# One joined product of v and state, and the q decay split over two engines

## The reference

```
def step(S, qkv_c):                       # one chunk: T = 128 tokens, D = 64
    qi, ki, vi = qkv_c
    scores = einsum('bhtd,bhsd,hts->bhts', qi, ki, mask)   # mask: exp(-s(t-s')) for t >= s', else 0
    intra  = einsum('bhts,bhsd->bhtd', scores, vi)
    cross  = einsum('bhtd,ht,bhde->bhte', qi, lam_t, S)    # lam_t = exp(-s t)
    o = scale * (intra + cross)
    kv = einsum('bhtd,ht,bhte->bhde', ki, lam_rev, vi)
    return (lam_T * S + kv, o)
out = rmsnorm(rmsnorm(outs, norm_w), proj_norm_w) @ weight_quant(proj_w).T
x + out * silu(ffn(layernorm(x)))
```

## Time and profile before

| | |
|---|---|
| median of 3 timed runs | 1314.46 us (1314.1 to 1314.81) |
| profiled execution, span | 1314.2 us; no time of its own is recorded beside the span |
| busy | PE 1289.1, DVE 1008.4, ACT 617.4, POOL 600.4 us |
| granted TensorE clock | full (2.4 GHz) in all 40 slices |

### The profile page before, as it was taken

How to read it: one execution, slowest core, us unless ns; L and a number is a source line. 1 busy time by engine, 2 the same in 40 slices (tenths; PEclk the granted TensorE clock), 3 DMA queues, 4 the chain that set the end, 5 groups by cost and what they waited for, 6 DMA issues and landing times.

```text
span 1314.2 us, 25908 instructions
## 1 busy us (share of the span) xinstructions
PE 1289.1 (98%) x10263; PEld 824.8 (63%) x10263; DVE 1008.4 (77%) x1567; ACT 617.4 (47%) x1216; POOL 600.4 (46%) x537
## 2 busy tenths in 40 slices
PE   4999999999999999999999999999999999999998
PEld 2577767675665757566574656657566575756655
DVE  7888367687676887878788787877878788787755
ACT  5884144344434635446354544644436363544621
POOL 1442785955354435354432535435333443535352
PEclk9999999999999999999999999999999999999999
DMA  9631101203012030210303011030300304021020
GB/s 361 248 97 66 57 34 37 101 33 106 1 38 100 17 121 18 76 46 18 121 17 120 18 57 65 17 121 18 94 28 19 119 17 121 17 58 49 1 65 32
DMA packets 33433, 90.32 MB, mean 69 GB/s; under 512 B 10529, under 2 KB 10785, under 8 KB 33314
## 3 DMA queue, kind: packets, MB, share of 16 engines
q1 hardware_dynamic: 33024, 88.65, 20.0%
q10 hardware_dynamic: 290, 0.02, 0.0%
HBM read 71.85 MB, written 16.81 MB: 67 GB/s over the span
## 4 chain that ended last, share of the span: by engine, by line
PE 94%; DVE 2%; ACT 2%; DMA 1%; issue 1%; SPq 0%; POOL 0%; DVEq 0%; ACTq 0%; POOLq 0%
PE ring L854 20%; PE ring L787 13%; PE ring L813 13%; PE ring L839 12%; PE ring L1012 10%; PE ring L988 5%; PE att_ps L892 4%; PE att_ps L942 4%; PE att_ps L938 4%; PE ring L904 2%; PE att_ps L919 2%; PE ring L867 1%; PE ring L754 1%; DMA raw<-in_ffn_w 1%; ACT junk L1951 1%
## 5 line engine op out<-in xcount | busy, mean ns | idle before, releaser
L854 PE MATMUL ring<-b_lo,qkv_q 128*128 128x256 f16 x1216 | 268.2, 272 | 0.0
L854 PE MATMUL ring<-b_hi,qkv_q 128*128 128x256 f16 x1216 | 268.2, 273 | 0.0
L2532 POOL TENSOR_TENSOR xt<-xt,gate_even 128x512 f32<-128x512 f32 x58 | 90.6, 1564 | 172.5 <-DVE gate_even L1626 131.8
L854 PEld LDWEIGHTS ring<-b_hi,qkv_q 128*128 128x128 fp8e4 x1216 | 120.2, 99 | 15.8 <-issue 0.4
L854 PEld LDWEIGHTS ring<-b_lo,qkv_q 128*128 128x128 fp8e4 x1216 | 118.9, 98 | 15.6
L2506 POOL TENSOR_TENSOR sq<-sq,cols 128x1024 f32<-128x1024 f32 x29 | 55.0, 1896 | 126.8 <-DVE b_lo L1423 118.6
L2094 ACT ACTIVATE gate_even<-gate_even 128x512 f32<-128x512 f32 x60 | 37.3, 625 | 136.2 <-DVE gate_even L1454 136.1
L942 PE MATMUL att_ps<-arena 128*64 128x128 f32 x1024 | 95.0, 273 | 0.0
L938 PE MATMUL att_ps<-arena 128*64 128x128 f32 x896 | 88.5, 276 | 0.0
L1523 DVE TENSOR_TENSOR arena<-att_ps,mask 128x512 f32<-128x512 f32 x128 | 79.3, 680 | 11.0 <-PE att_ps L892 11.0
L2385 POOL TENSOR_TENSOR ln<-ln,small 128x3 f32<-128x3 f32 x32 | 37.4, 1168 | 100.2 <-DVE ln L1311 99.3
(11 more groups left out here) (298 smaller groups left out, 3523.1 us busy)
## 6 DMA issues: line engine op xcount, KB each, us to landing
xt<-in_x SPq DMA_DIRECT2D x60, 512.0 KB, 3.7
out<-xt SPq DMA_DIRECT2D x31, 512.0 KB, 2.7
raw<-in_qkv_w SPq DMA_DIRECT2D x24, 512.0 KB, 15.8
y<-in_x_turned SPq DMA_DIRECT2D x14, 512.0 KB, 5.9
y_odd<-in_x_turned SPq DMA_DIRECT2D x14, 512.0 KB, 6.7
raw<-in_ffn_w SPq DMA_DIRECT2D x8, 512.0 KB, 9.8
norm_rows<-norm_out SPq DMA_DIRECT2D x14, 256.0 KB, 6.0
raw<-in_proj_w SPq DMA_DIRECT2D x6, 512.0 KB, 4.7
```

Source lines behind the costliest of these rows:

```text
L854: ins = pe.matmul(ring[:, b, e * BT:(e + 1) * BT], qkv_q[:, cb, o:o + P], part[:, cb, :], start=(cb == 0 and part is b_hi and (e == 0 or i ...
L2532: pool.tensor_tensor(o, o, gate_of(i)[:, c, cs], ALU.add).then_inc(s_add, 1)
```

## The change

The product of a chunk's head is cut along its tokens. For the first 64 tokens t only the first 64 source tokens count (the mask is zero elsewhere), so 64 rows of masked scores and 64 rows of decayed q fill one operand of 128 rows: the stationary operand is v of the first 64 tokens above the head's state (`v_state`), the moving one a `stack`. The same stationary operand serves the last 64 tokens with zeros over the decayed q. Then one product of v (128 rows) by the scores of the last 64 tokens (64 columns) is added. So a head takes one product of 128 columns and one of 64, in place of two of 128.

With it:

- state and decayed q of every head lie in partitions 64 to 127. The q decay is one operation of 64 x 1024 for the even heads on VectorE (new, 28 of them) and one for the odd heads on GpSimd; both need the outputs of the chunk before to be done.
- the state decay is one operation of 64 x 1024 on GpSimd.
- the masks are still four operations a chunk, cut by token halves instead of by e; the first of each pair covers 64 partitions.
- v of the first 64 tokens is copied into `v_state` by a DMA of 64 x 1024 f32 that ScalarE issues (28 of them), and outputs wait for it.
- `b_turned` gets a place of its own, and the waits that came with the shared place go.

```
@@ tensor_program, outputs
-                if not is_first(g):
-                    pe.wait_ge(s_ql, HALF * takes_over(g) + half + 1)
-                    if half == 0:
-                        pe.wait_ge(s_st, 2 * passes_on(g))
+                if not is_first(g) and half == 0:
+                    pe.wait_ge(s_ql0, takes_over(g) + 1)
+                    pe.wait_ge(s_ql, takes_over(g) + 1)
+                    pe.wait_ge(s_st, 2 * passes_on(g))
+                    pe.wait_ge(s_vcopy[c], copied(i, c))
...
                 for j in range(CPH):
                     r = half * CPH + j
-                    if not is_first(g):
+                    to = [att_ps[e * D:(e + 1) * D, half, j, :].rearrange("p (s t) -> p s t", s=2) for e in range(2)]
+                    v = [v_tok[:, c, r * P + e * D:r * P + (e + 1) * D] for e in range(2)]
+                    if is_first(g):
                         for e in range(2):
-                            pe.matmul(att_ps[e * D:(e + 1) * D, half, j, :],
-                                      state[:, passes_on(g) % 2, r, e * D:(e + 1) * D], q_decay[:, r, :],
-                                      start=True, stop=False, skip_group_check=True)
+                            ins = pe.matmul(to[e], v[e], stack[:, e, r, 0:2, :], start=True, stop=True)
+                        continue
+
                     for e in range(2):
-                        ins = pe.matmul(att_ps[e * D:(e + 1) * D, half, j, :],
-                                        v_tok[:, c, r * P + e * D:r * P + (e + 1) * D],
-                                        scores_m[:, half, e, j, :], start=is_first(g), stop=True,
-                                        skip_group_check=True)
+                        pe.matmul(to[e], joined(g)[:, r, e, :], stack[:, e, r, 0:3:2, :],
+                                  start=True, stop=False, skip_group_check=True)
+                    for e in range(2):
+                        ins = pe.matmul(to[e][:, 1, :], v[e], stack[:, e, r, 1, :],
+                                        start=False, stop=True, skip_group_check=True)
@@ vector_program
+            def decay_q(i, c):
+                g = chunk(i, c)
+                if is_first(g):
+                    return
+                dve.wait_ge(s_q, CPH * (i + 1))
+                if takes_over(g) == 0:
+                    dve.wait_ge(s_tables, TABLES)
+                dve.wait_ge(s_o, HALF * g)
+                q, by = (of.rearrange("p r (s t) -> p r s t", s=2)
+                         for of in (q_t[0:D, :, c * T:(c + 1) * T], lam_q[0:D, :, :]))
+                dve.tensor_tensor(stack[D:P, 0, :, 0:3:2, :], q, by, ALU.mult).then_inc(s_ql0, 1)
...
@@ mask_scores
-                if c == 0 and i > 0 and by_products(i - 1):
-
-                    dve.wait_ge(s_ops, of_o_product(i - 1, "p3"))
+                early = slice(0, P if is_first(g) else D)
...
-                    for e in range(2):
-                        dve.tensor_tensor(scores_m[:, half, e, :, :], att_ps[:, 2 * half + e, :, :],
-                                          mask[:, e, half * CPH:(half + 1) * CPH, :], ALU.mult).then_inc(s_scm, 1)
+                    for s, rows in enumerate((early, slice(0, P))):
+                        ts = slice(s * D, (s + 1) * D)
+                        dve.tensor_tensor(stack[rows, :, hs, s, :], att_ps[rows, 2 * half:2 * half + 2, :, ts],
+                                          mask[rows, :, hs, ts], ALU.mult).then_inc(s_scm, 1)
@@ vector_program, attention_by_tokens(i, 0)
                     go_on_z12(i)
                     take_z11(i)
+                    decay_q(i, 1)
                     return
@@ vector_program, before attention_by_tokens
+                decay_q(i, 0)
                 if not is_last(chunk(i, 0)):
                     decay_k_tokens(i, 0)
@@ scalar_program
+            def copy_v(i, c):
...
+                for by in v_at(i, c):
+                    act.wait_ge(*by)
+                if g > 1:
+                    act.wait_ge(s_o, HALF * (g - 1))
+                else:
+                    act.wait_ge(s_wout, w_n["qkv", QKV_TILES - 1])
+                act.dma_start(joined(g)[0:D, :, :, :].rearrange("p r e d -> p (r e d)"),
+                              v_tok[0:D, c, :]).then_inc(s_vcopy[c], DMA)
@@ gpsimd_program
-                pool.tensor_tensor(q_decay[:, hs, :], q_t[:, hs, c * T:(c + 1) * T], lam_q[:, hs, :],
-                                   ALU.mult).then_inc(s_ql, 1)
...
+                pool.tensor_tensor(stack[D:P, 1, :, 0:3:2, :], q, by, ALU.mult).then_inc(s_ql, 1)
...
-                for e in range(2):
-                    rows, cs = slice(e * D, (e + 1) * D), slice(e * D, (e + 1) * D)
-                    pool.tensor_tensor(state[rows, (n + 1) % 2, :, cs], state[rows, n % 2, :, cs],
-                                       lam_T[rows, :].unsqueeze(2).to_broadcast([D, PR, D]), ALU.mult).then_inc(s_sd, 1)
...
+                to, of = (v_state[D:P, k % 2, :, :, :].rearrange("p r e d -> p (r e) d") for k in (n + 1, n))
+                pool.tensor_tensor(to, of, lam_T[D:P, :].unsqueeze(2).to_broadcast([D, H, D]),
+                                   ALU.mult).then_inc(s_sd, 1)
```

More of the change, by code:

```diff
@@ L160, in program @@
         diag = sb("diag", [P, CHUNKS, T])
+        with nc.sbuf_tensor("b_turned", [P, CHUNKS, NCB, T], F32) as b_turned:
+            pass
+        o_row = sb("o_row", [P, CPH, T])
+        o_split = sb("o_parts", [P, 3, 2, CPH, T], F16)
         wsum = diag[:, 0, 0:5 * NCB]
@@ L197, in program @@
         s_ident, s_iota, s_cut = sem("ident_made"), sem("iotas_made"), sem("mask_cut")
-        s_state0 = sem("state_zeroed")
+        s_zeros = sem("stack_zeros_set")
+        s_vcopy = [sem(f"v_copied{c}") for c in range(CHUNKS)]
         s_ones, s_peak = sem("constants_set"), sem("peak_taken")
@@ L336, in is_last, with decays @@
             return g % NCHUNK == NCHUNK - 1
+        def decays(g):
+            return sum(not is_first(k) and not is_last(k) for k in range(g + 1))
         def passes_on(g):
@@ L347, in of_half, with copied, joined @@
             return chunk(i, c) * HALF + h + 1
+        def copied(i, c):
+            return DMA * sum(not is_first(chunk(k, c)) for k in range(i + 1))
+        def joined(g):
+            return v_state[:, passes_on(g) % 2, :, :, :]
         def of_ffn(i, c, h):
@@ L1559, in add_state @@
                 else:
-                    dve.wait_ge(s_sd, 2 * (passes_on(g) - (g // NCHUNK + 1)) + 2)
+                    dve.wait_ge(s_sd, decays(g))
                 for e in range(2):
-                    rows, cs = slice(e * D, (e + 1) * D), slice(e * D, (e + 1) * D)
-                    to = state[rows, (n + 1) % 2, :, cs]
+                    rows = slice(e * D, (e + 1) * D)
+                    to = v_state[D:P, (n + 1) % 2, :, e, :]
                     if is_first(g):
@@ L2004, in weigh_b @@
             def weigh_b(i, c):
-                act.wait_ge(s_o, HALF * (chunk(i - 1, 1) + 1))
+                if c == 0 and i > 2:
+                    act.wait_ge(s_bslo, of_b_sum(i - 1, "S4"))
+                    if by_products(i - 2):
+                        act.wait_ge(s_ops, of_o_product(i - 2, "p3"))
                 act.wait_ge(s_yn, of_turned(i, c))
@@ L2473, in decay_q @@
                     return
[L2474 to L2477 removed]
+                pool.wait_ge(s_q, CPH * (i + 1))
+                if takes_over(g) == 0:
                     pool.wait_ge(s_tables, TABLES)
[L2479 to L2482 removed]
+                pool.wait_ge(s_o, HALF * g)
+                if c == 1:
+                    pool.wait_ge(*((s_zeros, 1) if i == 0 else (s_vwsum, 3) if i == 1 else (s_zbias, HALF * (i - 1))))
+                elif i + 1 == NB:
+                    pool.wait_ge(s_gamma, chunk(i - 1, 1) + 1)
+                elif by_products(i - 1):
+                    pool.wait_ge(s_beta, chunk(i + 1, 1) + 1)
+                else:
+                    pool.wait_ge(*((s_pwsum, 1) if i == BY_PRODUCTS - 1 else (s_add, of_out(i - 1, 1, 1))))
+                q, by = (of.rearrange("p r (s t) -> p r s t", s=2)
+                         for of in (q_t[D:P, :, c * T:(c + 1) * T], lam_q[D:P, :, :]))
+                pool.tensor_tensor(stack[D:P, 1, :, 0:3:2, :], q, by, ALU.mult).then_inc(s_ql, 1)
+                pool.wait_ge(s_ql, takes_over(g) + 1)
             def decay_state(i, c):
```

79 lines of the change are left out of this document (43 added, 36 removed).

## The result

The changed kernel took 1330.91 us in the median of 4 runs (1327.91 to 1334.76), the kernel before 1314.63 beside it: ratio 1.0125 [1.0104, 1.0146]. A later repeat of the same pair (x_after_again) gave 1.0152 [1.0124, 1.018]. The sign was forecast and the size was not: +16 us where +6.6 was expected, 2 us outside the range. The profiled execution has a span of 1333.5 us, 19.3 above the 1314.2 of before. It is the longest of the four runs (1334.76 us). They come in two pairs: 1327.91 and 1328.92 us with a mean granted clock of 1.000, 1332.91 and 1334.76 us with 0.997. The kernel before is at 1.000 wherever it was timed beside a run of the experiments.

What follows compares the result with a forecast made beforehand. TensorE, 98% busy, was taken to bound the kernel, with two VectorE chains without slack. Terms: -20.0 + 10.8 + 12.8 + 1.0 + 2.0 = +6.6 us on 1314.46, so 1321 us; range 1307 to 1329.

Steps and rivals of the forecast that it cites:

- TensorE's saving: Outputs of 28 chunks: eight steps dropped, eight narrowed to 64 columns at 0.129 us each, saving 20.0 us (0 to 24.4).
- Chain A: VectorE's slackless work up to the last v product: even-chunk decay makes TensorE wait 1.2 us in 9 blocks, 10.8 us.
- Chain B: VectorE's masks before the odd chunk's total: decay adds 1.6 us in 8 blocks, 12.8, plus 1.0 in blocks 4, 8, 12.
- the sign that I had set for being wrong: The forecast of a slower kernel would be wrong if the odd chunk's decay before the masks took 1.2 us in most blocks.
- Blocks 0 to 3: Early blocks: one new decay each in 2 and 3 at 1.0 us, 2.0 together (0 to 4); nothing in 0 and 1.
- the exclusion: VectorE operations with two SBUF inputs and GpSimd's stand while the other runs; charged in the decay waits before v and masks.
- 98% busy: TensorE's share of the span, read as only less TensorE work or an instruction too late for it moving the end.
- The copy: Rival: the even chunk's v copy lands late, taking over 5.1 us; 1329 to 1336 us, chance 0.12.
- Narrow steps save: Rival claimed the opposite: weight loads make 64-column steps save nothing, leaving the waits alone; 1334 to 1341 us, chance 0.03.
- The port free in B: Rival: the odd chunk's decay before the masks costs only its own length; 1306 to 1311 us, faster, chance 0.22.
- VectorE did not absorb its decays: Rival claimed the opposite: VectorE's 23% idle takes in all the new work; 1294 us, at best 1290, chance 0.05.

Runs made afterwards that it cites:

- x_no_odd: Changed kernel with 7 of 8 head pairs left out of GpSimd's q decay from block 2 on, VectorE's whole: 1324.31 us, 1.0074 of the kernel before.
- x_none: Changed kernel with 7 of 8 head pairs left out of both engines' q decays from block 2 on: 1307.11 us, 0.9927 of the kernel before.
- x_block2_lock: x_block2, with GpSimd's product of the even chunk's state waiting from block 3 on until VectorE has added v: 1316.74 us, 1.0007 of the kernel before.
- x_block2: Changed kernel with VectorE's even-chunk q decay in block 2 moved behind the second `add_v`: 1332.19 us, 1.0116 of the kernel before.
- x_no_even: Changed kernel with 7 of 8 head pairs left out of VectorE's q decay from block 2 on, GpSimd's whole: 1313.17 us, 0.9974 of the kernel before.
- x_best: x_block2_lock with odd decay behind the gate's z22, GpSimd's state product waiting for it, and block 1's outputs' scale before its last v-weight sum: 1316.69 us, 1.0007.
- x_best_even: x_best with the even chunk's decay also moved behind its masks: 1319.84 us, 1.003 of the kernel before.
- x_block2_even: x_block2 with the even chunk's decay moved behind its masks from block 3 on: 1318.30 us, 1.0011 of the kernel before.
- x_block2_odd: x_block2 with the odd chunk's VectorE decay moved behind the masks: 1321.83 us, 1.0036 of the kernel before.

## Why the prediction missed

**TensorE's saving: right, a little small.** A narrow step took 0.117 us, not 0.129; the outputs of a chunk went from 3.544 to 2.728 us, 28 x 0.815 = 22.8 us for 20.0. In the trace after, one pair of heads follows the other by 0.335 us, a wide step of 0.218 and a narrow one of 0.117.

**Chain A: right.** Predicted 10.8; the blocks from 5 on stall 12.2 us, of which 2.1 were there before. The rule of the Trainium skill ("SBUF — State Buffer", Who interferes with whom) and the trace agree: 2.81 us for a 1.2 us operation behind GpSimd, 1.22 with GpSimd held off.

**Chain B: right in sum, wrong in the order in most blocks.** Predicted 12.8 and 1.0; measured 10.2 and 2.8. I had VectorE wait for GpSimd's L2510. It did in blocks 7 and 11 (a decay of 2.2 us, a stall of 1.93 for the 1.6 predicted). In blocks 5, 6, 9, 10, 13 and 14 VectorE came first by 0.05 us, its decay took 1.22 us, and it was GpSimd that waited, and TensorE for GpSimd's sum (1.06 each). So the sign that I had set for being wrong, a decay of 1.2 us in most blocks of B, did come, and the kernel was slower all the same: it overlooked that GpSimd's sum is wanted by the same matmul. That the total came out near the 13.8 is partly luck.

**Blocks 0 to 3: the step that failed.** The prediction put it as "one new decay each before L1399; I take 1.0 us each, 2.0, between 0 and 4" and nothing for blocks 0 and 1. Comparing starts of each chunk's scores in the two traces, the changed kernel is 1.66 us late at block 2, 8.94 at its odd chunk and 9.74 at block 4, though TensorE had by then saved 7 x 0.815 = 5.7: 15.4 us were lost where I had 2.0, 11.3 in blocks 2 and 3 and 4.1 in blocks 0 and 1. From block 4 on it loses 9.5 more net, 26.6 against the 17.1 saved there; predicted 24.6. So 13.4 too little was charged in front and 2.0 behind (a scale and an `o_lo` wait at the ends of sequences, 1.0 us each), and 2.8 too little was put down as saved: 13.4 + 2.0 - 2.8 = 12.6, by which +6.6 missed the +19.2 of the profiled span.

I priced block 2 by its instruction count. What stood beside it were GpSimd's fp8 sums of weights, 3.8 to 4.7 us each. Their rows were in the trace of before, with a VectorE product stretched to four times its 1.2 us beside one of them, in the very block (GpSimd and VectorE, kernel before):

```profile
234.89 4.69 POOL L2442 TENSOR_TENSOR k_sum_last<-qkv_q,k_sum 128x2048 fp8e4<-128x2048 fp8e4 x1
```

```profile
235.93 4.73 DVE L1335 TENSOR_TENSOR y<-y,norm_rows 128x1024 f32<-128x1024 f32 x1
```

And I had already charged the exclusion in chain A. Which engine comes first decides (x_no_odd), and in the changed kernel VectorE came late: its first product of block 2 waited 2.1 us for a load that was issued at 229.17 instead of 226.16. The traces show where those 3.0 us come from. The load waits, by way of a DMA, for GpSimd's second `norm_pair` there, which was done 3.0 us later (220.39, not 217.38). GpSimd was 2.0 us late when it came to it, 1.7 of them because VectorE's L1662, for which its scale waits, came that much later, and 1.0 us is the exclusion once more, beside VectorE's `o_lo` (changed kernel; the same GpSimd operation took 0.22 us before):

```profile
219.15 1.24 POOL L2446 TENSOR_SCALAR norm_pair<-ln 128x1 f32<-128x1 f32 x1
```

```profile
219.09 1.23 DVE L1626 TENSOR_TENSOR o_lo<-ow,o_hi 128x1024 f16<-128x1024 f32 x1 [1.37 <-ACT o_hi L2202]
```

And an idle TensorE lost 2.5 us more by its clock, a price I had nowhere.

The median of the timed runs missed by less than the profile, +16.3 instead of +19.2, since two of its four runs kept full clock. Those two, 13.3 and 14.3 us above the kernel before, lie inside the stated range. So it was partly luck on which side of 1329 the median fell; the mis-sized term stands either way.

**What stays lost in x_none.** In its profile it still gives back 13.0 of 22.8 us. Of these 7.1 are the decays after all: 4.4 in block 2 (exclusion and clock) and 2.7 in block 1, where they are whole (GpSimd's decay begins later and takes 3.14 instead of 2.50 us, and behind it stand a weight sum and then the scale that L990 needs). Some 3 are the ends of sequences and block 3, 2.2 chain A, which has no slack for an earlier TensorE. So "98% busy" did not mean that TensorE's time is the kernel's time: even with hardly any decay 5 of 22.8 us went into chains that had been timed to it within half a microsecond.

**The rivals.** The copy is hidden in the changed kernel (2.9 us in most blocks, 4.3 at most); in x_block2_lock it once took 6.08 us, and TensorE stood 0.96. Narrow steps save. The port free in B was half true (VectorE did not wait in six of eight blocks) and gained little, since GpSimd is on the same path. VectorE did not absorb its decays.

**Open.** What decides whether TensorE's clock falls after the wait of 2.2 to 2.4 us in block 1: it did in four profiles and did not in seven. Where the runs of x_block2 at 0.997 lost the rest of their clock. And what block 2 looked like in the two runs of the changed kernel at 1.000.

## What to carry to other kernels

Before moving an elementwise operation, list what the other elementwise engine has running at that place and how long each of its instructions is: the price of an operation with two SBUF inputs is up to its neighbour's whole length, and it falls on whichever of the two comes second, be it by a few hundredths of a microsecond. Ask it for every block that differs from the steady one; set-up work such as weight sums makes the early blocks the dearest. Where two such operations collide, one semaphore wait that orders them can be worth more than the instruction itself (14 us here), but each new order has to be looked at for the next collision. And TensorE's saved time counts only as far as every chain timed to it has slack; check each of them, not the tightest two.

## What the runs showed of the hardware

- VectorE and GpSimd excluded each other for whole instructions at every size seen: 3.14 us for 128 elements per partition beside a 4.69 us sum, 1.61 for a single column beside a decay. The one that came second stood, in either direction: a decay of 4.07 us beside a sum in the changed kernel, a decay of 1.22 and a sum of 4.87 where the decay came 0.04 us first (x_no_odd). It also held `b_lo` (scalar_tensor_tensor, two SBUF inputs); masks with an input from PSUM ran at 0.6 us each beside GpSimd.
- From 100 us on: after TensorE waits of 5.33, 4.41 and 2.52 us in block 2 (changed kernel, x_no_even, x_none) and 3.83 in block 1 (x_best, x_best_even) the next 8 to 13 matmuls followed at 0.427 us, the 1.2 GHz level. After the wait of 2.2 to 2.4 us in block 1 the clock fell in four profiles (x_block2, x_block2_even, x_block2_odd, x_block2_lock) and not in seven others; after waits of 1.8 us and less it never did. The wait alone does not tell.
- A copy of 64 partitions x 4 KB within SBUF landed in 2.9 us in most cases, and in up to 6.08 us (x_block2_lock).
